# Spreading the first layer-norm statistics of the second sequence over the feed-forward stage of the first

## The reference, cut to what matters

```python
def _layernorm(x, axis=-1, eps=1e-5):
    m = jnp.mean(x, axis=axis, keepdims=True)
    v = jnp.var(x, axis=axis, keepdims=True)
    return (x - m) / jnp.sqrt(v + eps)

xn = _layernorm(x, axis=-1)
s = attention(xn)      # q, k, v of width 128; softmax(q k^T / sqrt(128)) v; mask; w_o
g = _silu(ffn(xn))     # 1024x1024 weight quantised to int4 steps, + bias + rank-16 product
x = x + s * g
```

## Time and profile before

| | us |
|---|---|
| two timed runs | 1223.58 and 1282.17, median 1252.87 |
| the profiled execution | 1220.31 |
| its span on core 4, the slowest | 1218.8 |
| spans of the 8 cores in it | 1205.8 to 1218.8 |

### The profile page before, as it was taken

One profiled execution on the slowest core, in us unless ns is written; L12 is line 12 of the kernel. 1 busy time (PEld: TensorE's weight loads), 2 busy tenths in 40 slices (PEclk: granted clock), 3 DMA queues, 4 the chain that ended last, 5 costly groups with the idle time before them and its releaser, 6 DMA issues.

```text
span 1218.8 us, 12473 instructions; the slowest of 8 cores (1205.8 to 1218.8 us)
## 1 busy us (share of the span) xinstructions
PE 937.6 (77%) x4453; PEld 508.0 (42%) x4453; DVE 431.9 (35%) x664; ACT 350.6 (29%) x678; POOL 21.8 (2%) x30
## 2 busy tenths in 40 slices
PE   0755767868775889889894789788885888979795
PEld 0422324546554334333332444366664333443342
DVE  2646644334332122131305565423332023132303
ACT  1322425444551211201111343455452110112110
POOL 4010000000000000000000000000000000000000
PEclk9987887988886999898998799999997989999998
DMA  5440210000002115144032330000001114123032
GB/s 142 135 144 33 87 35 18 1 18 18 18 18 70 35 35 171 36 118 160 27 111 103 119 124 1 1 1 1 1 1 69 35 35 154 53 71 137 2 137 104
DMA packets 25311, 78.54 MB, mean 64 GB/s; under 512 B 3601, under 2 KB 6673, under 8 KB 25250
## 3 DMA queue, kind: packets, MB, share of 16 engines
q1 hardware_dynamic: 18338, 52.57, 13.6%
q10 hardware_dynamic: 4608, 16.78, 3.4%
q0 software_dynamic: 2304, 8.39, 2.2%
HBM read 60.95 MB, written 16.78 MB: 64 GB/s over the span
## 4 chain that ended last, share of the span: by engine, by line
PE 58%; DVE 15%; ACT 13%; issue 6%; DMA 6%; DVEq 0%; POOL 0%; ACTq 0%; SPq 0%; POOLq 0%
PE PA L163 45%; PE PS L163 7%; PE PF L163 6%; ACT A_sb L209 4%; ACT xfh L200 3%; DMA y<-xq 3%; DVE xfl L425 3%; ACT ATf L200 3%; DVE nm L235 3%; DVE g_sb L195 2%; DVE xq L190 2%; DMA wstpair<-kern 1%; DVE ssum L235 1%; DVE kq_y L190 1%; DVE kdd L190 1%
## 5 line engine op out<-in xcount | busy, mean ns | idle before, releaser
L163 PE MATMUL PA<-xfh,q_sb 128*128 128x512 bf16 x512 | 202.3, 395 | 7.0 <-ACT g_sb L209 3.6
L163 PE MATMUL PA<-xfl,q_sb 128*128 128x512 bf16 x512 | 201.0, 393 | 0.0
L209 ACT ACTIVATE g_sb<-PA,invsc 128x512 f32<-128x512 f32 x64 | 43.7, 687 | 279.7 <-PE PA L163 201.5
L163 PE MATMUL PA<-ATf,Vt 128*128 128x256 f32 x512 | 114.4, 382 | 12.3 <-ACT ATf L200 12.3
L209 ACT ACTIVATE A_sb<-PS,nmax 128x512 f32<-128x512 f32 x128 | 86.2, 685 | 115.0 <-DVE nmax L235 115.0
L425 DVE TENSOR_TENSOR xfl<-PF,xfh 128x1024 bf16<-128x1024 f32 x32 | 39.2, 1225 | 224.8 <-ACT xfh L200 224.8
L163 PEld LDWEIGHTS PA<-ATf,Vt 128*128 128x128 f32 x512 | 97.2, 191 | 31.0 <-issue 18.0
L235 DVE TENSOR_REDUCE nm<-PS 128x1 f32<-128x512 f32 x128 | 81.5, 685 | 28.1 <-PE PS L163 28.1
L163 PEld LDWEIGHTS PA<-xfh,q_sb 128*128 128x128 bf16 x512 | 51.8, 101 | 87.2 <-issue 37.9
L163 PE MATMUL PS<-Kh,Qh 128*128 128x512 bf16 x128 | 55.9, 437 | 41.5 <-ACT A_sb L209 41.5
L163 PE MATMUL PF<-identf,xn_tm 128*128 128x128 f32 x256 | 45.6, 336 | 51.6 <-DVE xfl L425 41.2
(11 more groups left out here) (135 smaller groups left out, 1171.8 us busy)
## 6 DMA issues: line engine op xcount, KB each, us to landing
wstpair<-x SPq DMA_DIRECT2D x64, 512.0 KB, 4.9
y<-xq ACTq DMA_DIRECT2D x32, 512.0 KB, 5.5
xq<-x SPq DMA_DIRECT2D x30, 512.0 KB, 5.3
wstpair<-kern POOLq DMA_DIRECT2D x16, 512.0 KB, 3.9
Vt<-x SPq DMA_DIRECT2D x2, 512.0 KB, 14.8
wstpair<-wq SPq DMA_DIRECT2D x1, 512.0 KB, 6.1
wstpair<-wk SPq DMA_DIRECT2D x1, 512.0 KB, 5.0
wstpair<-wv SPq DMA_DIRECT2D x1, 512.0 KB, 4.2
```

What stands on the lines that cost most here:

```text
L163: e.matmul(o, l, r, start=st, stop=sp, is_transpose=t))
L209: e.activation(o, i, f, bias=b, scale=s, accum_out=a)),
```

## The change

`emit_prefetch_loads` is replaced by `emit_prefetch_pair(k)` and `emit_prefetch_stats()`. Pair 0 (the two loads into `xq` slots 2 and 3) is issued at the end of `it == 1`, pair 1 (the two loads into `Vt`) at the end of `it == 2`. Right behind each load come its sum on DVE and its square on ScalarE. All four squares write to `xn_tm[2]` and `xn_tm[3]`, each waiting for the one before. At the end of `it == 4` the small operations that make mean and deviation follow, and the normalisation of the first two blocks. `seq_program(1)` takes these over and normalises only blocks 2 and 3 itself. Nothing is added to or taken from the work in total.

```diff
         def emit_ln_loads_stats(qt):
+            if qt == 0 and pre is not None:
+                stats_tok[0] = pre["stats"]
+                return
             srcs = [xbuf[SLOT[tb4]] for tb4 in range(4)]
             extra = None
-            if qt == 0 and pre is not None:
-                sq_toks = pre["lds"]
-                srcs = pre["srcs"]
-                extra = pre["afree1"]
-            elif s == 0 and qt == 0:
+            if s == 0 and qt == 0:
...
         def emit_ln_xn(qt, half):
             if qt == 0 and pre is not None:
...
+                if half == 0:
+                    ln_toks[0][0] = pre["ln01"][0]
+                    ln_toks[0][1] = pre["ln01"][1]
...
+                else:
+                    for tb4 in (2, 3):
+                        sl = SLOT[tb4]
+                        ln_toks[0][tb4] = xn_pre(
+                            tb4, pre["src23"][tb4 - 2],
+                            pre["ld23"][tb4 - 2], "vector",
+                            stats_tok[0], i=sl, stb=sb0 + tb4)
                 return
...
-        def emit_prefetch_loads():
+        prestg = {"lds": [], "sums": [], "sq_last": None}
+
+        def emit_prefetch_pair(k):
             row0n = (s + 1) * S
+            sb0n = (s + 1) * NTB
             srcs = [xbuf[2], xbuf[3], Vt[:, 0:1024], Vt[:, 1024:2048]]
...
+            for tb4 in (2 * k, 2 * k + 1):
                 r = row0n + tb4 * 128
                 w = W(xbuf_free[SLOT[tb4]]) if tb4 < 2 else W(state["AT_free"])
...
+                t_ld = load(srcs[tb4], x_hbm[r:r + 128, :], waits=w)
+                prestg["lds"].append(t_ld)
+                col = slice(sb0n + tb4, sb0n + tb4 + 1)
+                t_sum = vred(ssum[:, col], srcs[tb4], Alu.add, waits=[t_ld])
+                t_sq = act(xn_tm[2 + tb4 % 2][:, :], srcs[tb4], Act.Square,
+                           accum=ssq[:, col],
+                           waits=W(t_ld, xntm_free[2 + tb4 % 2],
+                                   afree1, prestg["sq_last"]))
+                prestg["sq_last"] = t_sq
+                prestg["sums"].append((t_sum, t_sq))
+
+        def emit_prefetch_stats():
...
+            t1 = ts1("vector", smean[:, c0:c0 + 4], ssum[:, c0:c0 + 4],
+                     1.0 / D, Alu.mult, waits=[sums[-1][0], sums[-1][1]])
...
+            for tb4 in range(2):
+                t_xn = ts2("vector", xn_tm[2 + tb4][:, :], srcs[tb4],
...
+                           waits=W(t7, lds[tb4], sq_last, afree1))
+                ln01.append(t_xn)
...
-            if s + 1 < SEQ_PER_CORE and it == 2:
-                emit_prefetch_loads()
+            if s + 1 < SEQ_PER_CORE:
+                if it in (1, 2):
+                    emit_prefetch_pair(it - 1)
+                elif it == NQT:
+                    emit_prefetch_stats()
```

More of the change, by code:

```diff
@@ L484, in emit_ln_xn @@
             if qt == 0 and pre is not None:
[L485 to L491, removed]
+                if half == 0:
+                    ln_toks[0][0] = pre["ln01"][0]
+                    ln_toks[0][1] = pre["ln01"][1]
+                    xbuf_free[2] = pre["ln01"][0]
+                    xbuf_free[3] = pre["ln01"][1]
+                else:
[5 more added lines that the diff above has]
+                            stats_tok[0], i=sl, stb=sb0 + tb4)
                 return
@@ L837, in emit_sgtp_stores @@
             xf_free[j] = (gparts[qt][0], gparts[qt][1])
-        def emit_prefetch_loads():
+        prestg = {"lds": [], "sums": [], "sq_last": None}
+        def emit_prefetch_pair(k):
             row0n = (s + 1) * S
+            sb0n = (s + 1) * NTB
             srcs = [xbuf[2], xbuf[3], Vt[:, 0:1024], Vt[:, 1024:2048]]
-            lds = []
-            for tb4 in range(4):
+            prestg["srcs"] = srcs
+            afree1 = state["A_free2"][1]
+            for tb4 in (2 * k, 2 * k + 1):
@@ L844, in emit_prefetch_loads @@
                 r = row0n + tb4 * 128
                 w = W(xbuf_free[SLOT[tb4]]) if tb4 < 2 else W(state["AT_free"])
-                lds.append(load(srcs[tb4], x_hbm[r:r + 128, :], waits=w))
-            state["pre1"] = {"srcs": srcs, "lds": lds,
-                             "afree1": state["A_free2"][1]}
+                t_ld = load(srcs[tb4], x_hbm[r:r + 128, :], waits=w)
+                prestg["lds"].append(t_ld)
+                col = slice(sb0n + tb4, sb0n + tb4 + 1)
+                t_sum = vred(ssum[:, col], srcs[tb4], Alu.add, waits=[t_ld])
@@ new lines, in emit_prefetch_pair @@
+                t_sq = act(xn_tm[2 + tb4 % 2][:, :], srcs[tb4], Act.Square,
[5 more added lines that the diff above has]
+        def emit_prefetch_stats():
+            srcs = prestg["srcs"]
+            lds = prestg["lds"]
+            sums = prestg["sums"]
+            sq_last = prestg["sq_last"]
+            afree1 = state["A_free2"][1]
+            sb0n = (s + 1) * NTB
+            c0 = sb0n
+            t1 = ts1("vector", smean[:, c0:c0 + 4], ssum[:, c0:c0 + 4],
+                     1.0 / D, Alu.mult, waits=[sums[-1][0], sums[-1][1]])
+            t2 = ts1("vector", svar[:, c0:c0 + 4], ssq[:, c0:c0 + 4],
+                     1.0 / D, Alu.mult, waits=[t1])
+            t3 = tt("vector", stmp[:, 0:4], smean[:, c0:c0 + 4],
+                    smean[:, c0:c0 + 4], Alu.mult, waits=[t2])
+            t4 = tt("vector", svar[:, c0:c0 + 4], svar[:, c0:c0 + 4],
+                    stmp[:, 0:4], Alu.subtract, waits=[t3])
+            t5 = act(svar[:, c0:c0 + 4], svar[:, c0:c0 + 4], Act.Ln,
+                     bias=epsb[:, 0:1], waits=[t4, t_eps])
+            t6 = act(srstd[:, c0:c0 + 4], svar[:, c0:c0 + 4], Act.Exp,
+                     scale=-0.5, waits=[t5])
+            t7 = stt("vector", snmr[:, c0:c0 + 4], smean[:, c0:c0 + 4], -1.0,
+                     srstd[:, c0:c0 + 4], Alu.mult, Alu.mult, waits=[t6])
+            ln01 = []
+            for tb4 in range(2):
+                t_xn = ts2("vector", xn_tm[2 + tb4][:, :], srcs[tb4],
+                           smean[:, sb0n + tb4:sb0n + tb4 + 1],
+                           srstd[:, sb0n + tb4:sb0n + tb4 + 1],
+                           Alu.subtract, Alu.mult,
+                           waits=W(t7, lds[tb4], sq_last, afree1))
+                ln01.append(t_xn)
+            state["pre1"] = {"stats": t7, "ln01": ln01,
+                             "src23": srcs[2:], "ld23": lds[2:]}
```

## The result

The changed kernel is slightly slower. Its median is 1226.23 us over 43 runs, that of the kernel before 1222.27 us over 42; the ratio, over the undisturbed executions of both, is 1.0035, 95% interval 1.0026 to 1.0045, so +4.3 us. The profiled execution took 1224.14 us, with a span of 1222.6 on its slowest core, core 0. (In some timings a part of the cores ran at a lower granted clock for long stretches; "undisturbed executions" are those left when executions over 1.5% above the fastest of their kernel, or with one half of the chip over 1% longer than the other, are set aside, and "undisturbed cores" are those whose mean clock in the execution was over 0.90.)

A forecast was written before the change was run, and what follows sets the result against it. The bound was taken to change by stage: the statistics chain at the seam, ScalarE's queue at the ends of `it` 1 and 2. -4.9 + 2.7 + 3.1 + 1.7 = +2.6 us gave 1222.9, likeliest 1223, range 1214 to 1238.

The forecast's parts named there:

- What bounds the three places: At the seam, the chain of statistics; at the ends of `it` 1 and 2, ScalarE's queue, which TensorE waits for next.
- The seam, -4.9: Between the sequences: small operations directly follow the last output block, so normalisation and transposes start 4.9 us earlier.
- The end of `it` 2, +2.7: Pair 1's squares, the second waiting for its load, delay the first Silu; chunk 2 starts 2.7 us later.
- The end of `it` 1, +3.1: Pair 0 lands at about 477.1 and 479.1; its squares delay the Silu, and chunk 2 starts 3.1 us later.
- The clock, +1.7: Matmuls at the lower clock behind the new TensorE gap at `it` 1 lose 1.7 us; at `it` 2 0 is added.
- the spell is already paid: At `it` 2 the lower clock already follows today's 1.63 us gap, so 0 is added, with 1.7 us as bound.
- The sum, +2.6: Whole kernel: -4.9 + 2.7 + 3.1 + 1.7 = +2.6 us, against the profiled execution's 1220.31.
- Hidden after all: Loads land before ScalarE reaches them at both places and the clock holds: net -0.9 us, 1219.4; chance 0.2.
- Loads late: Both pairs land 2 to 3 us later than by spacing, with longer clock spells: about +9, 1230; chance 0.18.
- Table switches: Squares between Silus need their own function set: 4 table loads on ScalarE, +5.1 us, 1228; chance 0.02.
- No gain at the seam: A held-up store or load stands right behind the seam, so the 4.9 us shrinks to 0: 1228; chance 0.05.
- the section that it names: Trainium skill's "What ACT_TABLE_LOAD costs": 1.28 us plus a 1.38 us drain per load; the trace was said to show no drain.

The follow-up runs named there:

- the filler: The changed kernel with 16 matmuls of 512 columns, whose result nobody reads, ahead of chunk 2 at `it` 1 and 2: 1219.76 us, ratio 0.999 to before.

## Why the prediction was right or wrong

- **What bounds the three places: right.** The gaps ahead of chunk 2 are released by the Silu, the Silu stands behind the squares, most of the second squares at `it` 1 are released by a load, and the seam shortens by what stood in it. Moving only the squares, and moving only the loads, both show it.
- **The seam, -4.9: right.** -4.8 on average over 8 cores, and the group behind it moved with it (+0.15 to the end).
- **The end of `it` 2, +2.7: right.** +2.8. The first square starts 14.7 us after the loop's start and the Silu 17.3; on core 4 the prediction's times come to 14.8 and 17.5. Pair 1 landed near the old places of the `xq` loads, and not where the `Vt` loads landed before. That the mean of 8 cores fits a working from one core so closely is in part luck: the gap's growth lies between 1.8 and 3.5 us when single cores are set against the mean before.
- **The end of `it` 1, +3.1: a little low.** +3.65. The spacing of 2.0 us between the landings was right (the two squares start 2.0 us apart on average, though 2.85 on core 0). What was low is where they start: the step left ScalarE's stores where they were, and with the two loads in the queue the last store comes 0.9 us later on average (13.4 us after the loop's start in place of 12.5).
- **The clock, +1.7: this is the step that failed.** It measured +3.9: the loops lost 3.9 us beyond the gaps, and the filler gave back 5.2 us of the whole. The step took one spell of the smaller size at `it` 1, and at `it` 2 added nothing, since "the spell is already paid". That was so on core 4, the profiled one. Of the other seven only core 7 had one there; with gaps of 3.1 to 4.8 us all 8 cores of the changed kernel do. A spell that one core has by its gap of 1.6 us isn't paid on the others. By loop the loss beyond the gaps is 2.3 us at `it` 1, where 1.7 was forecast, and 1.6 at `it` 2, where it was 0.
- **The sum, +2.6: too small by this term.** With the last two terms at their measured sizes it is -4.8 + 2.8 + 3.65 + 3.9, about +5.5, near the difference of the mean spans (1212.2 to 1217.3, +5.2). The kernel's time, which goes by the slowest core, rose by 4.3, so +2.6 has three fifths of it. The predicted 1223 is 3.2 below the measured 1226.2.
- **The reference of the number.** The sum was set on the profiled execution, 1220.31 us. The median shown, 1252.87, was that of two runs, one of them at 1282.17; 40 more put it at 1222.27. Set against 1252.87 the predicted number would read as 2.4% faster, which no term of the sum says: the sum forecasts slightly slower, and that is what came.
- **The rivals.** *Hidden after all* failed at its condition: both loads were there before ScalarE on 1 of 8 cores at `it` 1 and on 4 of 8 at `it` 2, and the clock didn't hold. *Loads late* came in part: the second square at `it` 1 started 0.6 us later than predicted on average and 1.9 us on core 0, short of the 2 to 3 of that case, but its other half, more time at the lower clock behind the longer gaps, came. *Table switches* didn't come: no table load stands beside the squares. *No gain at the seam* fell. Of the two points on which the prediction has the trace disagree with the section that it names, only the drain is one; that Square and Silu would need a load between them was its own supposition.

## What to carry to other kernels

Work moved out of a gap that everyone waits in is only a gain if the place where it goes is looked at as an in-order queue: ask what stands behind it on that engine, and put it where the engine is idle for longer than the work and its inputs have long landed. Here one Silu in each 4.5 us of matmuls left 3.8 us for a square that took 1.04 of them, while in front of the first Silu there were 0.2. Loads moved to a busy place also push back the stores beside them: here by 0.7 us. A stall on TensorE costs its own length and, behind it, matmuls at the lower clock; price that by all cores of the trace and not by the profiled one.

## What the runs showed of the hardware

The lower clock behind a wait was dearer than expected: 6.45 us more of waiting in two places, with mean waits of 3.7 and 4.0 us, brought 3.9 us of further loss. The length of a wait alone doesn't tell whether the clock falls behind it. At `it` 2 of the kernel before it was at 0.78 and 0.76 in the 7 us behind the waits of 1.63 and 1.47 us (cores 4 and 7), and at 1.00 behind the wait of 1.79 us (core 1). Keeping TensorE busy with 16 matmuls that nobody needs made the kernel 5 us faster than leaving it idle (1213.6 against 1218.9 us, mean over cores), though TensorE's useful work went on only 0.4 to 0.6 us sooner.
